# The first two conv1 jobs of a patch tokenizer moved into the last step of its weight stage, and the store of the low weights cut in eight

## The reference, cut to what matters

```python
# x (16, 3, 112, 112) -> 784 patches of 3 x 16 x 16
x = (x - mean) / (1e-06 + std) / sqrt(16)
x = conv2d(x, conv1_w, conv1_b)                      # 3 -> 64 channels, 3 x 3
residual = x
x = gelu(group_norm(x, gn1_g, gn1_b, groups=32))
x = conv2d(x, rconv1_w, rconv1_b)                    # 64 -> 64
x = gelu(group_norm(x, gn2_g, gn2_b, groups=32))
x = conv2d(x, rconv2_w, rconv2_b)                    # 64 -> 64
x = residual + x
x = conv2d(x, proj_w, proj_b, stride=16, pad=0)      # -> 192 features a patch
x = x + row_emb[...] + col_emb[...]
...                                                  # attention block, then a block of attention and MLP
```

## Time and profile before

| | us |
|---|---|
| median of 3 runs | 1534.28 |
| lowest and highest | 1529.33, 1537.36 |
| the profiled execution, its own time | 1532.89 |
| its span, first to last instruction | 1531.1 |
| PE busy in the span | 1387.3 |
| DVE, ACT, POOL busy | 1117.0, 862.5, 584.9 |

### The profile page before, as it was taken

The page is one execution under the profiler, slowest core; times in us unless marked ns, Lnnn a source line. Parts: engine busy times, 40 slices in busy tenths (PEclk is TensorE's granted clock), DMA queues, the critical chain, the costliest instruction groups (busy, mean ns, idle before and its releaser), DMA issues. The chain is left out here.

```text
span 1531.1 us, 43872 instructions
## 1 busy us (share of the span) xinstructions
PE 1387.3 (91%) x14066; PEld 1024.4 (67%) x14066; DVE 1117.0 (73%) x4207; ACT 862.5 (56%) x2126; POOL 584.9 (38%) x1114
## 2 busy tenths in 40 slices
PE   3999959888999899899999998999899795988889
PEld 1877523334887588668957885888588595564646
DVE  5753338999888888888888888888888743384710
ACT  1334426777767676676776766767676601424442
POOL 1000025555454545454554454454444401241500
PEclk9999979999999999999999999999999997967999
DMA  7899863334554555455545554554555598100000
GB/s 210 243 258 260 226 242 101 98 100 128 143 143 130 138 146 136 107 155 141 143 123 145 142 143 112 148 140 130 141 142 140 154 271 176 32 1 1 2 4 12
DMA packets 124565, 206.95 MB, mean 135 GB/s; under 512 B 19964, under 2 KB 88124, under 8 KB 123774
## 3 DMA queue, kind: packets, MB, share of 16 engines
q1 hardware_dynamic: 124414, 204.89, 49.3%
HBM read 103.70 MB, written 21.30 MB: 82 GB/s over the span
## 5 line engine op out<-in xcount | busy, mean ns | idle before, releaser
L540 PE MATMUL rc<-sb_acts,sb_rwd 128*64 128x512 f16 x1764 | 560.8, 390 | 21.8 <-DMA sb_acts<-sb_hst 21.7
L541 PE MATMUL rc<-sb_acts,sb_rwd 128*64 128x512 f16 x1764 | 561.9, 391 | 0.0
L394 POOL TENSOR_TENSOR sb_tmp<-sb_mst,sb_half_neg 128x8 f32<-128x8 f32 x200 | 354.6, 1773 | 472.1 <-DVE sb_mst L858 472.1
L469 ACT ACTIVATE sb_f32q<-c,sb_gsh,sb_gsc 128x128 f32<-128x128 f32 x792 | 299.0, 459 | 286.1 <-POOL sb_gsh L404 286.1
L540 PE MATMUL rc<-sb_acts,sb_rwl 128*64 128x512 f16 x1176 | 362.1, 390 | 5.2 <-issue 5.2
L541 PE MATMUL rc<-sb_acts,sb_rwl 128*64 128x512 f16 x1176 | 361.6, 389 | 0.0
L619 PE MATMUL pj<-sb_wall_arena 128*64 128x384 f16 x1792 | 304.1, 334 | 6.9 <-DVE sb_wall_arena L877 6.6
L477 ACT ACTIVATE sb_g2f<-rc,sb_gsh,sb_gsc 128x128 f32<-128x128 f32 x784 | 298.1, 483 | 4.5 <-POOL sb_gsh L404 4.5
L623 PEld LDWEIGHTS pj<-sb_wall_arena 128*64 128x64 f16 x1792 | 219.3, 223 | 66.8
L623 PE MATMUL pj<-sb_wall_arena 128*64 128x192 f16 x1792 | 239.4, 245 | 0.0
L540 PEld LDWEIGHTS rc<-sb_acts,sb_rwd 128*64 128x64 f16 x1764 | 179.0, 110 | 87.4 <-DMA sb_acts<-sb_hst 32.6
(11 more groups left out here) (167 smaller groups left out, 1907.3 us busy)
## 6 DMA issues: line engine op xcount, KB each, us to landing
sb_acts<-sb_hst SPq DMA_DIRECT2D x792, 78.8 KB, 2.6
sb_im<-x_planes SPq DMA_DIRECT2D x202, 136.5 KB
sb_wall_arena<-w_lo SPq DMA_DIRECT2D x48, 528.0 KB, 3.8
sb_acts<-sb_hst SPq DMA_DIRECT2D x96, 162.0 KB, 3.1
sb_wall_arena<-w_lo SPq DMA_DIRECT2D x24, 480.0 KB, 3.6
sb_f32q<-in_proj SPq DMA_DIRECT2D x12, 576.0 KB, 4.5
sb_wall_arena<-in_proj SPq DMA_DIRECT2D x12, 576.0 KB, 5.5
w_lo<-sb_wall_arena SPq DMA_DIRECT2D x1, 6144.0 KB, 20.8
```

Source lines behind the costliest of these rows:

```text
L394: ch.did(gp.tensor_tensor(t1, var, half_neg[:, :], ALU.pow))
L469: ins = nc.scalar.activation(g1f[:, q * Q + m, :], c1[q][:, m * HALF:(m + 1) * HALF], ACT.Gelu, bias=gsh[q][:, m:m + 1], scale=gsc[q][:, m ...
L540: nc.tensor.matmul(out[0:CH, :], w_odd, x_odd, start=(n == 0), stop=(n == 14))
L541: yield nc.tensor.matmul(out[CH:128, :], w_even, x_even, start=(n == 0), stop=(n == 14))
```

## The change

PE splits the last pair of steps off its loop: after step 22 it runs conv1 of jobs 0 and 1, and in step 23 the means of both between the two halves. The tails of all steps write pj twice and a half-bank of rc[1 - p][1] in place of c1[0], c1[1] and pj, so c1 is free for the two jobs; PE therefore waits for the evacuation of the step before ahead of half 1 and for its low half ahead of the tail. ACT runs gelu1 of job 0 between its two copies of step 23 and gelu1 of job 1 behind the evacuation. DVE widens the parameters before its loop, takes statistics, moments and means of jobs 0 and 1 ahead of the low halves of step 23, and puts split1 of job 0 between these. POOL clears acts[1] between norm 1 and norm 2. On SP the zero planes go out in iteration 20, the wait for the planes and the first two im2col loads stand in iteration 22; behind the loop load_im(2, 0) comes before the copies of jobs 0 and 1, and store_t(23) behind them. The low weights are stored in eight DMAs of 768 KB, one after the copies of each of the units 1 to 8; SP, ACT and DVE wait for all eight where they waited for the one.

```diff
@@ -51,6 +51,7 @@
...
 MID = 48
+LOW_STORES = 8
@@ -257,6 +258,12 @@
...
+            def load_im(u, p):
...
@@ -269,24 +276,17 @@
...
                         store_piece(C + m)
-            sp.wait_ge(s_zero, 1)
-            for n, k in ((NPAT, U), (NPAT + U, U), (NPAT + 2 * U, U), (NPAT + 3 * U, 1)):
...
-            def load_im(u, p):
...
-            sp.wait_ge(s_scr, 16 * STORES)
-            load_im(0, 0)
-            load_im(1, 1)
+                if n == 20:
+                    sp.wait_ge(s_zero, 1)
+                    for m, k in ((NPAT, U), (NPAT + U, U), (NPAT + 2 * U, U), (NPAT + 3 * U, 1)):
+                        for at, planes in ((0, 12), (12, 6)):
+                            sp.dma_start(bass.AP(tensor=scr, offset=at * PLANE + m * PAD, ap=[[PLANE, planes], [1, k * PAD]]),
+                                         zt[0:planes, 0:k * PAD]).then_inc(s_scr, 16)
+                if n == 22:
+                    sp.wait_ge(s_scr, 16 * STORES)
+                    load_im(0, 0)
+                    load_im(1, 1)
             store_t(FU - 2)
-            store_t(FU - 1)
-            sp.wait_ge(s_wlo, 2 * FU)
-            sp.dma_start(wlod.ap(), b1[:, 0:HALF * E]).then_inc(s_wst, 16)
@@ -307,7 +307,7 @@
...
                 if not first:
-                    sp.wait_ge(s_wst, 16)
+                    sp.wait_ge(s_wst, 16 * LOW_STORES)
@@ -315,16 +315,22 @@
...
                         double(2 * u + 3, 1 - p, 1)
+                        if first and 1 <= u <= LOW_STORES:
+                            n = HALF // LOW_STORES * E
+                            sp.dma_start(wlod.ap()[:, (u - 1) * n:u * n], b1[:, (u - 1) * n:u * n]).then_inc(s_wst, 16)
...
-            double(0, 0, 0)
...
             load_im(2, 0)
+            sp.wait_ge(s_tps, FU - 1)
+            double(0, 0, 0)
             double(1, 0, 1)
+            store_t(FU - 1)
+            sp.wait_ge(s_wlo, 2 * FU)
@@ -411,12 +417,13 @@
...
             gp.memset(hfull[:, :].bitcast(F32), 0.0).then_inc(s_zl, 1)
-            for p in range(2):
-                pool.wait_ge(s_tps, FU - 1 + p)
-                gp.memset(acts[p][:, 2, :].bitcast(F32), 0.0).then_inc(s_zl, 1)
+            pool.wait_ge(s_tps, FU - 1)
+            gp.memset(acts[0][:, 2, :].bitcast(F32), 0.0).then_inc(s_zl, 1)
...
             norm(1, 1, False)
+            pool.wait_ge(s_tps, FU)
+            gp.memset(acts[1][:, 2, :].bitcast(F32), 0.0).then_inc(s_zl, 1)
@@ -432,9 +439,11 @@
...
-            def fold_step(i, p, first, more=True):
+            def fold_step(i, p, first, more=True, last=False):
...
                 for q in range(2):
+                    if last and q == 1:
+                        gelu1(0, 0, False)
@@ -444,10 +453,20 @@
...
                 act.wait_ge(s_tps, n + 1)
-                for k, bank in enumerate((c1[0], c1[1], pj)):
+                for k, bank in enumerate((pj[:, 0:192], pj[:, 192:384], rc[1 - p][1][:, 0:192])):
                     nc.scalar.activation(tev[p][:, :, 3 * P * k:3 * P * (k + 1)],
-                                         bank[:, 0:192].rearrange("p (n e) -> p e n", e=Q),
+                                         bank.rearrange("p (n e) -> p e n", e=Q),
                                          ACT.Copy, scale=1.0 / (WS * WS)).then_inc(s_tev, 1)
+            def gelu1(k, q, guard=True):
...
@@ -457,18 +476,9 @@
...
                     fold_step(i, p, False)
-            for p in range(2):
-                fold_step(FU // 2 - 1, p, False, False)
-            def gelu1(k, q, guard=True):
...
+            fold_step(FU // 2 - 1, 0, False, False)
+            fold_step(FU // 2 - 1, 1, False, False, True)
+            gelu1(1, 1, False)
@@ -505,10 +515,8 @@
...
             act.sem_inc(s_g2, 4)
-            gelu1(0, 0, False)
-            gelu1(1, 1, False)
             group(0, 0, True)
-            act.wait_ge(s_wst, 16)
+            act.wait_ge(s_wst, 16 * LOW_STORES)
@@ -560,34 +568,32 @@
...
-            def fold_step(i, p, first):
+            def fold_step(i, p, first, last=False):
...
                         pe.wait_ge(s_wlo, 2 * (n - 2) + q + 1)
+                    if q == 1 and not (first and p == 0):
+                        pe.wait_ge(s_tev, 3 * n)
...
                     run(conv).then_inc(s_fold, 1)
+                    if last and q == 0:
+                        means(0, 0)
+                        means(1, 1)
                 if not (first and p == 0):
-                    pe.wait_ge(s_tev, 3 * n)
+                    pe.wait_ge(s_wlo, 2 * n)
                 v = acts[p][:, :, 0:U * PAD].rearrange("p h (q r x) -> p h q r x", q=2, r=SL)
-                for k, bank in enumerate((c1[0], c1[1], pj)):
+                for k, bank in enumerate((pj[:, 0:192], pj[:, 192:384], rc[1 - p][1][:, 0:192])):
...
                         for h in range(2):
-                            last = nc.tensor.matmul(bank[TP * h:TP * h + TP, 0:192], w,
+                            done = nc.tensor.matmul(bank[TP * h:TP * h + TP, :], w,
...
                                                     start=(m == 0), stop=(m == 2))
-                last.then_inc(s_tps, 1)
-            pe.wait_ge(s_wprep, W_READY)
-            for p in range(2):
-                fold_step(0, p, True)
-            with pe.Fori(1, FU // 2) as i:
-                for p in range(2):
-                    fold_step(i, p, False)
+                done.then_inc(s_tps, 1)
@@ -607,6 +613,20 @@
...
                 last.then_inc(s_st, 1)
+            pe.wait_ge(s_wprep, W_READY)
+            for p in range(2):
+                fold_step(0, p, True)
+            with pe.Fori(1, FU // 2 - 1) as i:
+                for p in range(2):
+                    fold_step(i, p, False)
+            fold_step(FU // 2 - 1, 0, False)
+            pe.sem_inc(s_c1, 1)
+            pe.wait_ge(s_w1s, 192)
+            pe.wait_ge(s_im[0], 32)
+            conv1(0, 0)
+            conv1(1, 0)
+            fold_step(FU // 2 - 1, 1, False, True)
@@ -633,6 +653,9 @@
...
                 pe.wait_ge(s_g2, 2 * u + q + 1)
+                if first and p == 1 and q == 0:
+                    pe.wait_ge(s_wlo, 2 * FU)
+                    pe.wait_ge(s_rowz, 4)
@@ -686,24 +709,16 @@
...
-            pe.sem_inc(s_c1, 1)
...
             pe.sem_inc(s_pj, 1)
-            pe.wait_ge(s_w1s, 192)
-            pe.wait_ge(s_im[0], 32)
-            pe.wait_ge(s_tev, 3 * FU)
-            pe.wait_ge(s_wlo, 2 * FU)
-            conv1(0, 0)
-            conv1(1, 0)
-            means(0, 0)
-            means(1, 1)
...
             conv1(0, 1)
-            pe.wait_ge(s_rowz, 4)
...
             conv1(1, 1)
+            pe.wait_ge(s_tev, 3 * FU)
+            pe.wait_ge(s_rowz, 2)
@@ -747,9 +762,9 @@
...
-            def w_lo(i, p):
+            def w_lo(i, p, halves=(0, 1)):
                 n = 2 * i + p
-                for q in range(2):
+                for q in halves:
@@ -801,11 +816,6 @@
...
                 fold_pair(i)
-            with dve.Fori(5, FU // 2 - 1) as i:
-                fold_pair(i)
-            for p in range(2):
-                w_lo(FU // 2 - 1, p)
@@ -820,14 +830,14 @@
...
             ins.then_inc(s_padz, 1)
-            dve.wait_ge(s_tps, FU)
-            dve.wait_ge(s_padz, 3)
-            dve.wait_ge(s_scr, 16 * STORES)
-            dve.wait_ge(s_zl, 3)
+            with dve.Fori(5, FU // 2 - 1) as i:
+                fold_pair(i)
+            w_lo(FU // 2 - 1, 0)
...
             v.sem_inc(s_sp2, 2)
-            for t in acts:
+            def rows_zeroed(t):
@@ -923,14 +933,23 @@
...
             read_means(1, 1)
+            w_lo(FU // 2 - 1, 1, (0,))
+            dve.wait_ge(s_tps, FU - 1)
+            rows_zeroed(acts[0])
+            dve.wait_ge(s_zl, 2)
             split1(0, 0, 0, None)
+            w_lo(FU // 2 - 1, 1, (1,))
...
             split1(1, 1, 0, None)
+            dve.wait_ge(s_tps, FU)
+            rows_zeroed(acts[1])
+            dve.wait_ge(s_zl, 3)
+            dve.wait_ge(s_scr, 16 * STORES)
             group(0, 0, True)
-            dve.wait_ge(s_wst, 16)
+            dve.wait_ge(s_wst, 16 * LOW_STORES)
```

More of the change, by code:

```diff
@@ L258, in store_piece @@
                                  xhl[:, 6 * (k % 2) + q, :]).then_inc(s_scr, 16)
+            def load_im(u, p):
+                for up in range(2):
+                    sp.dma_start(im[p][54 * up:54 * up + 54, 0:RUN],
+                                 bass.AP(tensor=scr, offset=u * (U * PAD) + up * WD,
+                                         ap=[[1, 3], [PLANE, 18], [1, RUN]])).then_inc(s_im[p], 16)
             for n in range(FU):
@@ L271, in _ @@
                         store_piece(C + m)
-            sp.wait_ge(s_zero, 1)
-            for n, k in ((NPAT, U), (NPAT + U, U), (NPAT + 2 * U, U), (NPAT + 3 * U, 1)):
-                for at, planes in ((0, 12), (12, 6)):
-                    sp.dma_start(bass.AP(tensor=scr, offset=at * PLANE + n * PAD, ap=[[PLANE, planes], [1, k * PAD]]),
```

(35 more changed lines are left out.)

## The result

The changed kernel took 1523.66 us (median of 8 runs, 1519.96 to 1530.97), the kernel before, run beside it, 1534.32 (8 runs). The ratio is 0.9931, 95% interval 0.9909 to 0.9954: 10.7 us faster, where 15.5 were forecast. The profiled execution took 1521.87 with a span of 1520.1, 11.0 shorter than the earlier trace rows.

The account below looks back on a forecast made before the run. Between 204 and 232.3 us a chain of engines, then 12.7 us of copies stuck behind the store, was taken to bound the kernel. 16.5 - 0.5 (clock) - 0.5 (stores) = 15.5 us gained: 1518.5 us, 8 in 10 within 1511 to 1526.

Parts of the forecast that it names:

- likeliest case: Whole kernel: gain of 12.5 to 19 us, 1515 to 1522 us, chance 0.75.
- first rival: Start of group 0: job 2's copies come late behind store_t(23) and an im2col load, 6 to 8 us lost, 1526; chance 0.14.
- signs of being wrong: Copies waited for after each piece, weight steps grown beyond 7.36 us, or job 0's end later than 218.
- the chain: Step 23 into job 0: means, norm, gelu, cast; third cast at 214.2 instead of 230.15, 16.5 us gained in all.
- conv1 of jobs 0 and 1 before step 23: End of weight stage: conv1 after step 22, im2col loads in iteration 22, step 23's copies still in time; cost 0.
- The clock: PE's gap at 206.6 to 209: a lower clock slows job 0's pairs; 0.5 us, between 0 and 1.5.
- The pieces: Group 0: eight store pieces queue ahead of im2col loads and copies; 0.5 us in all, bounds 0 to 20.8.
- the second rival: Group 0: the store pieces block the copies, 5.0 us each, 40 us lost, 1558 (1539 by ring order alone); chance 0.05.
- The third rival: Weight steps: ACT's evacuation comes late in all 22, 0.7 us each, gain gone, 1534; chance 0.06 including nothing moved.
- about 9 us: Kernel before, first job: chain DVE, PE, POOL, ACT, DVE from 206.62 to the cast ending at 214.83.

Follow-up runs that it names:

- filled wait: The changed kernel with 14 extra pairs of matmuls, read by nobody, ahead of step 23's wait for its copies; 1522.25 us, ratio 0.9911.
- spread rows: The changed kernel with im2col rows reordered so the loads' slowest dimension is 18 instead of 3, conv1's weights placed to match; 1502.69 us, ratio 0.9781.
- one tile late: The changed kernel with unit 1's im2col load moved behind the copies of step 23; 1518.68 us, ratio 0.9883.
- one store: The changed kernel with the low weights in one 6144 KB DMA behind the copies of jobs 0 and 1, instead of eight pieces; 1541.93 us, ratio 1.0025.
- the change again: The changed kernel measured once more without any edit, in the first batch of experiments; 1524.83 us, ratio 0.9919.
- the pieces alone: The kernel before with only the low-weight store cut in eight and moved into group 0, old order of first jobs; 1532.12 us, ratio 0.9982.

## Why the prediction was partly right

The sign, the mechanism and the range for 8 in 10 (1511 to 1526) held; the size was 4.8 us too large, and 1523.66 lies outside the 1515 to 1522 of the likeliest case, nearer to the first rival's 1526. Two of the prediction's own signs of being wrong came true: job 0 ended at about 221 instead of 215 (the sign says 218), and copies were waited for after each piece.

That the range held is partly luck. Behind group 0 the lead in the change's profile was 8.3 us, about half of what the chain alone was to give; another 4.3 came in groups 1 to 6, which the prediction had at nothing and no run explains.

**The step that failed** is "conv1 of jobs 0 and 1 before step 23", with its "Cost 0". It asked when SP could issue the loads and the copies, and there it was right to 0.2 us (190.19 against 190.35). It didn't ask what the loads do to the rings that the copies use. The earlier trace rows showed the same four loads with nothing behind them but stores, so that they made no copy wait at this place. In the change the slowest copy took 9.6 us to land instead of 3.0, and PE waited 3.91.

The loss splits as follows. Start-up moves the weight stage by up to 2.5 us from profile to profile, so the table counts from ACT's copy of step 22's first half (192.62 in the earlier trace rows) to the third cast (230.15). The forecast was 214.2 - 192.62 = 21.6. "Wait" is PE's in step 23; for the filled wait the 14 pairs at 0.217 us are added to 1.41. "Rest" is the third cast's delay against the spread version, less the wait, so it is what the wait doesn't explain.

| kernel | copy to third cast | wait | rest | clock, 196 to 206 |
|---|---|---|---|---|
| before | 37.5 | | | |
| forecast | 21.6 | 0 | | |
| spread rows | 21.4 | 0 | 0 | 1.00 |
| one tile late | 21.7 | 0.2 | 0.0 | 1.00 |
| one store | 24.0 | 2.5 | 0.1 | 1.00 |
| filled wait | 25.9 | 4.5 | 0.0 | 1.00 |
| the change again | 26.2 | 2.8 | 2.0 | 0.83 |
| the change | 28.2 | 3.9 | 2.8 | 0.71 |

So the chain that I worked out (means, norm, gelu, cast, two rounds) was right to 0.2 us, and the loss is the wait, with the slower clock on top in those executions where it fell: in the three rows with a wait and a clock of 1.00 nothing is left to explain, 0.1 us at most. In the change's profile nine pairs of half 0 and eight of half 1 run 0.43 us apart instead of 0.22, which is 3.6 us on PE; 2.8 of them reach the third cast. **The clock** term, 0.5 with bounds 0 to 1.5, was too small in those: 2.0 and 2.8 us. It was also sought at the wrong gap. In the change's profile the clock went to its lower level of 1.2 GHz (a granted clock of 0.50 in 201 to 203, 0.63 us a matmul instead of 0.38) during the 3.9 us in which PE had nothing; after 2.8 and 2.5 us of waiting it fell once, with a delay, and once not.

**The first rival** (job 2's copies behind store_t and an im2col load) happened at about a fifth of its price of 6 to 8 us: PE waited 1.94 us, the lead fell by 1.4; in the second profile by 0.3, with one tile late by 1.0, with spread rows not at all.

**The pieces.** 0.5 us were forecast. They cost 1.2 in the change (lead 9.5 to 8.3), 1.9 in its second profile, 1.6 in the kernel with the pieces alone, 0 with spread rows. Landing was 3.6 to 5.8 us, 3.7 in the median, as forecast but for the slowest. The margin of 2.0 us of the earlier trace rows, with which the second rival was answered, did not hold beside the narrow loads: PE waited 0.70 to 1.00 us for copies after each piece. That is less than the 2 us a piece at which this rival turns the sign, and of the 6.9 us only 1.2 were lost, as DVE sets the rhythm in group 0 (busy for 92.18 of 100 us). With spread rows there is no such wait, and with one store and narrow loads the lead changes by only 0.2 over the rest of group 0, so it takes both, pieces and narrow loads. In one piece the store costs 16.4 us of lead and turns the sign.

**The third rival** is out (PE 154.00 of 154 us).

**What stays open.** Between group 0 and the end of group 6 the change gains 4.3 us more over the kernel before (lead 8.3 to 12.6), in its second profile 1.8, with one tile late 3.1, with the pieces alone 0.7. The edit touches nothing there. PE's waits for copies vary in these groups as long as the loads are narrow (9.7 us in 9 times, against 13.4 in 17 before), so a shifted phase between copies and loads is a guess that fits; no run tests it.

In sum, in the change's profile, where the clock's 2.8 is the rest that the table leaves: 16.9 us of lead were forecast at the first statistics of rc. Less 3.9 for the wait and 2.8 for the clock, plus 0.6 for the earlier start (192.06 against 192.62) and 0.2 for the chain, that is 11.0, measured 10.95. Less 1.4 for job 2's copies and 1.2 for the pieces, plus the 4.3 gained later, that is 12.6 at the last cast. In the span 11.0 are left; the last part lost 1.6, as it did 0.8 and 1.4 in the profiles with one tile late and with spread rows, and 5.5 in the change's second profile. The prediction's "about 9 us" for the first job's chain is 8.2 by the two times that it names (206.62 to 214.83); the sum doesn't use it.

## What to carry to other kernels

When a DMA is moved ahead of others in a queue, price its time in the rings, not only its issue: count the entries of its slowest dimension, and read the DMA share of a stretch in which it runs alone (0.19 is three engines of sixteen). Here each narrow load ahead cost the slowest copy 1.4 to 1.7 us on average. A narrow load is cheap while nothing is behind it and dear in front of a wide copy that someone waits for. Before moving it, reshape it: here a new order of rows alone (0.9888) was worth more than the whole change (0.9931 and 0.9919), and with it the change gave some 14 us instead of 11 to 13 by the leads. And two stalls in a row are worth little one at a time: the cut store alone gave 4.4 us of lead and the early jobs alone lost 3.3.

## What was not expected of the hardware

The issue of a DMA is itself held back behind a large store. A copy takes SP about 0.60 us to issue; behind the 6144 KB store the eight copies above took 1.22 to 2.42 us each (median 1.39, 12.44 for the block), and three of the four of the earlier trace rows about 1.4. In the change, which has no such store, none of the 20 copies issued up to 235 us took more than 0.60. Single issues of up to 2.1 us occur elsewhere too, but not in a row. The four im2col loads were issued in the same 3.25 us whether they ran on three engines or on more (3.31), so SP's timeline gives no hint of how wide a transfer is. And in one execution of the same kernel the clock fell within the wait, in the other only some 0.7 us after PE had resumed (its matmuls go from 0.38 to 0.6 us at 202.5, behind a wait that ended at 201.84).
